# First layer of a four-layer graph network: base products kept turned for two node blocks, combined block by block

## The reference

```
weight = einsum('rb,bio->rio', w_comp, bases)      # 32 relations from 8 bases, 256 x 256 each
xw     = einsum('ni,rio->nro', h, weight)          # every node under every relation
msg    = xw[src, rel_type] * norm                  # one row of 256 per edge
out    = relu(segment_sum(msg, dst))
```

## Time and profile before

| | us |
|---|---|
| median of 3 runs | 6362.52 |
| lowest, highest | 6360.35, 6365.52 |
| span of the profiled execution | 6364.3 |

### The profile page before, as it was taken

The page is one execution under the profiler, slowest core; times in us unless marked ns, Lnnn a source line. Parts: engine busy times, 40 slices in busy tenths (PEclk is TensorE's granted clock), DMA queues, the critical chain, the costliest instruction groups (busy, mean ns, idle before and its releaser), DMA issues.

```text
span 6364.3 us, 77713 instructions
## 1 busy us (share of the span) xinstructions
PE 4985.1 (78%) x19175; PEld 3374.5 (53%) x19176; DVE 3946.2 (62%) x9442; ACT 1596.1 (25%) x3091; POOL 3597.4 (57%) x3549
## 2 busy tenths in 40 slices
PE   5999869999987777776666666279999997776766
PEld 3555547777773433333444444257787874333333
DVE  5555566666646666666666666876666665655555
ACT  3555534444440000001222222123333331000000
POOL 0000067777757777776777777223333335777776
PEclk8888889999997777777888887679999997667676
DMA  6999956666654444445777777267666774344343
GB/s 231 364 361 365 371 190 216 217 216 217 216 198 122 124 124 124 124 124 154 242 244 244 242 245 245 76 197 237 236 233 234 238 241 139 116 117 116 116 117 111
DMA packets 476381, 1279.57 MB, mean 201 GB/s; under 512 B 137938, under 2 KB 262716, under 8 KB 412533
## 3 DMA queue, kind: packets, MB, share of 16 engines
q1 hardware_dynamic: 315557, 832.27, 37.5%
q0 software_dynamic: 160464, 443.17, 24.2%
HBM read 636.68 MB, written 587.04 MB: 192 GB/s over the span
## 4 chain that ended last, share of the span: by engine, by line
PE 58%; DVE 11%; issue 10%; DMA 9%; POOL 6%; SPq 3%; ACT 1%; DVEq 1%; POOLq 0%; ACTq 0%
PE ps L1409 27%; PE ps L1584 11%; PE ps L1433 8%; PE ps L1567 5%; DMA table<-A 5%; POOL ring L630 3%; POOL A L630 2%; PE ps L1369 2%; DMA work<-place_dram 2%; DVE W L816 2%; DVE A L816 2%; PE ps L1384 1%; SPq L476 1%; SPq L355 1%; DMA A<-gat_table,ix 1%
## 5 line engine op out<-in xcount | busy, mean ns | idle before, releaser
L618 POOL DMA_INDIRECT ring<-table,idx x2490 | 2366.4, 950 | 1640.0 <-DVEq L840 774.8
L1409 PE MATMUL ps<-ring,W 128*128 128x256 f32 x3320 | 1189.5, 476 | 440.4 <-DVE W L816 278.0
L1409 PEld LDWEIGHTS ps<-ring,W 128*128 128x128 f32 x3320 | 683.3, 229 | 869.2 <-DVE W L816 399.6
L816 DVE TENSOR_SCALAR W<-iota,dloc,norm 128x128 f32<-128x128 f32 x1660 | 597.6, 361 | 766.7 <-PE ps L1409 756.8
L1409 PE MATMUL ps<-ring,A 128*128 128x256 f32 x1660 | 724.6, 543 | 271.5 <-DVE A L816 210.8
L643 POOL TENSOR_TENSOR ring<-ring,work 128x1024 f32<-128x1024 f32 x208 | 405.7, 1951 | 809.8 <-DMA ring<-rows_dram 809.8
L1584 PE MATMUL ps<-W_r,work_r 128*128 128x512 f32 x1960 | 701.1, 440 | 0.0
L834 DVE TENSOR_TENSOR X<-X,ps 128x256 f32 x1660 | 688.2, 415 | 17.2 <-PE ps L1409 15.2
L1409 PEld LDWEIGHTS ps<-ring,A 128*128 128x128 f32 x1660 | 340.2, 248 | 620.2 <-DVE A L816 367.6
L1433 PE MATMUL ps<-W_r,work_r 128*128 128x512 f32 x1568 | 560.0, 439 | 0.0
L1148 DVE TENSOR_TENSOR X<-X,ps 128x264 f32 x830 | 352.4, 425 | 329.4 <-PE ps L1567 272.8
(11 more groups left out here) (239 smaller groups left out, 7045.1 us busy)
## 6 DMA issues: line engine op xcount, KB each, us to landing
table<-A SPq DMA_DIRECT2D x294, 1024.0 KB, 6.2
ring<-rows_dram SPq DMA_DIRECT2D x208, 528.0 KB, 4.6
table<-A SPq DMA_DIRECT2D x49, 1280.0 KB, 5.4
table<-W SPq DMA_DIRECT2D x49, 1280.0 KB, 6.9
rows_dram<-ring SPq DMA_DIRECT2D x52, 1056.0 KB, 4.8
rows_dram<-A SPq DMA_DIRECT2D x52, 1056.0 KB, 4.6
ring<-table,idx POOLq DMA_INDIRECT x2490, 2.8
A<-W SPq DMA_DIRECT2D x264, 128.0 KB, 5.3
```

Of the source, the lines that this page charges most:

```text
L618: pool.indirect_dma_start(out=f_ring[:, s % NR, :], out_offset=None, in_=src, in_offset=bass.IndirectOffsetOnAxis(ap=idx[:, s:s + 1], axis ...
L816: return dve.tensor_scalar(marks_[:, k % G, :], iota[:, :], dloc[:, k:k + 1], norm[:, k:k + 1], ALU.is_equal, ALU.mult).then_inc(wk.onehot ...
L1409: pe.matmul(ps[:, s % banks, 0:D], marks_[:, s % G, :], f_ring[:, s % NR, :], start=True, stop=True).then_inc(wk.step_done, 1)
```

## The change

Two windows (called blocks) are taken together. The operands of the base product change sides: the bases are now stationary, 128 columns of them (8 bases x 2 strips of 8 output columns), and the transposed x of 256 nodes moves. The result has (strip, base, output column) along the partitions and nodes along the columns, so it is the stationary operand of the combination as it lies, and the sum over bases is along the partitions. The combination multiplies strips of 64 partitions (8 bases x 8 output columns) of one block by a 64 x 256 coefficient matrix (32 relations x 8 output columns); two strips stand beside one another. Its result has nodes along the partitions, in order. The `turns` t run over (pair of blocks, block, eighth of the output); a group of base products for the next pair follows every second turn. The split base products of nine groups are kept. There are two table tiles (A and XF); a whole one is stored in two transfers of 2 MB, with rows in node order. x comes in per pair of blocks. The seven index instructions become one.

```diff
+ OS = 8; CC = R0 * OS; OQ = D // (4 * OS); NSB = NWIN // 2; SLOTS = 9
+ l_table = [t[:, 0:R0 * D].rearrange("p (r o) -> p r o", r=R0) for t in (A, XF)]
+ L_TURNS = [(k, w, q) for k in range(NSB) for w in range(blocks_of(k)) for q in range(OQ)]
+ L_BASES = {L_AT[k, 0, 0] + (6, 8, 10, 12, 14, 16, 18, 20)[q]: (k + 1, q) for k in range(NSB - 1) for q in range(OQ)}
  # setup
- load(X[:, 0:NW1, :], x[0:NW1 * P].rearrange("(w p) c -> p w c", p=P))
-     load(comb_raw[i * BASES:(i + 1) * BASES, i // 4, i % 4 * R0:(i % 4 + 1) * R0], w_compT)
+     load(comb_row[i * OS:(i + 1) * OS, :], w_compT[i % BASES].partition_broadcast(OS))
- (six instructions on src_i, block_i, in_four, in_block)
+ ch(dve.scalar_tensor_tensor(idx[:, 0:KP], srcf[:, :], float(R0), types[:, walk0.tcol, :], ALU.mult, ALU.add))
  # SP
- sp.dma_start(l_S[k % 3][b:P:BASES, :].rearrange("i (g o) -> i g o", o=D), l_xb[:, b * D:(b + 1) * D])   # 8 per window
+ sp.dma_start(l_x[k % 2], x_rows[k]).then_inc(l_x_in[k % 2], 16)
+ def store_block(k, w):
+     t = L_AT[k, w, OQ - 1]
+     sp.wait_ge(l_act, t + 1)
+     sp.wait_ge(l_dve, t + 1)
+     for u in range(2):
+         sp.dma_start(rows[2 * k + w, u], (A, XF)[w][:, u * (R0 // 2) * D:(u + 1) * (R0 // 2) * D]).then_inc(l_t_free[w], 16)
  # VectorE (ScalarE alike: high_x, high_xb, and to_table of strip 0)
+ def low_xb(k, q):
+     m = OQ * k + q
+     dve.wait_ge(xb_high, m + 1)
+     dve.tensor_tensor(l_low[m % SLOTS], ps[:, 1 + m % 2, :]..., l_high[m % SLOTS]..., ALU.subtract).then_inc(xb_low, 1)
+ def to_table(t):
+     k, w, q = L_TURNS[t]
+     if q == 0 and k >= 1:
+         dve.wait_ge(l_t_free[w], 32 * k)
+     dve.wait_ge(l_full, 2 * t + 2)
+     dve.tensor_copy(table_place(t, 1), comb_bank(t, 1).rearrange("p (h r o) -> p h r o", h=2, o=OS)).then_inc(l_dve, 1)
+ for t, (k, w, q) in enumerate(L_TURNS):
+     to_table(t)
+     if t in L_BASES:
+         low_xb(*L_BASES[t])
+     if w == 0 and q == 4 and k + 1 < NSB:
+         low_x(k + 1)
  # PE
+ def base_products(k, q):
+     m = OQ * k + q
+     if q == 0:
+         pe.wait_ge(x_low, k + 1)
+     if m >= 2:
+         pe.wait_ge(xb_low, m - 1)
+     terms = [(b_high, l_xt_high, c) ...] + [(b_low, l_xt_high, c) ...] + [(b_high, l_xt_low, c) ...]
+     for h in range(2):
+         for n, (w, rows, c) in enumerate(terms):
+             ins = pe.matmul(ps[:, 1 + m % 2, h * 2 * P:(h + 1) * 2 * P], w[:, c, q, h, :], rows[k % 2][:, c, :], ...)
+ def combine(t):
+     k, w, q = L_TURNS[t]
+     u = (OQ * k + q) % SLOTS
+     if w == 0:
+         pe.wait_ge(xb_low, OQ * k + q + 1)
+     if t >= 2:
+         pe.wait_ge(l_act, t - 1)
+         pe.wait_ge(l_dve, t - 1)
+     terms = [(l_high, comb_high), (l_low, comb_high), (l_high, comb_low)]
+     for h in range(2):
+         for n, (rows, c) in enumerate(terms):
+             for s in range(2):
+                 part_ = slice(s * 64, (s + 1) * 64)
+                 ins = pe.matmul(comb_bank(t, s)[:, h * CC:(h + 1) * CC], rows[u][part_, h, w * P:(w + 1) * P], c[part_, :], ...)
+ for t, (k, w, q) in enumerate(L_TURNS):
+     combine(t)
+     if t in L_BASES:
+         base_products(*L_BASES[t])
+     if w == 0 and q == 3 and k + 1 < NSB:
+         turn_x(k + 1)
```

More of the change, by code:

```diff
@@ L126, in build @@
[L126 to L131, removed]
@@ L134, in build @@
+        assert 2 * CC == 512 and OQ == 8
         alpha = A[:, 0:NSC].rearrange("p (k h) -> p k h", h=HEADS)
@@ L352, in reorder_bank @@
[L352 to L369, removed]
@@ L370, in layer0_transfers, with load_x @@
-                for h in range(4):
-                    sp.wait_ge(l_t_free[h], 16 * NW1)
+                rows = table.rearrange("(w p) (t c) -> w t p c", p=P, t=2)
+                x_rows = x.rearrange("(k w p) c -> k p w c", p=P, w=2)
+                def load_x(k):
+                    if k >= 2:
+                        sp.wait_ge(l_turned, k - 1)
+                    sp.dma_start(l_x[k % 2], x_rows[k]).then_inc(l_x_in[k % 2], 16)
[5 more added lines that the diff above has]
+                        sp.dma_start(rows[2 * k + w, u], (A, XF)[w][:, u * (R0 // 2) * D:(u + 1) * (R0 // 2) * D]).then_inc(l_t_free[w], 16)
@@ L373, in head_loads @@
+                load_x(0)
+                load_x(1)
+                for k in range(NSB):
+                    if k + 2 < NSB:
+                        load_x(k + 2)
+                    for w in range(blocks_of(k)):
+                        store_block(k, w)
+                for w in range(2):
+                    sp.wait_ge(l_t_free[w], 32 * sum(blocks_of(k) > w for k in range(NSB)))
             def head_loads():
@@ L1208, in deviation @@
+                high_x(0)
+                act.wait_ge(b_split_low, 8)
+                for q in range(OQ):
+                    high_xb(0, q)
+                for t, (k, w, q) in enumerate(L_TURNS):
+                    to_table(t)
+                    if t in L_BASES:
+                        high_xb(*L_BASES[t])
+                    if w == 0 and q == 4 and k + 1 < NSB:
+                        high_x(k + 1)
             def deviation(g):
@@ new lines, in base_products @@
+                    terms = [(b_high, l_xt_high, c) for c in range(2)] + [(b_low, l_xt_high, c) for c in range(2)] + [(b_high, l_xt_low, c) for c in range(2)]
+                    for h in range(2):
+                        for n, (w, rows, c) in enumerate(terms):
+                            ins = pe.matmul(ps[:, 1 + m % 2, h * 2 * P:(h + 1) * 2 * P], w[:, c, q, h, :], rows[k % 2][:, c, :],
+                                            start=(n == 0), stop=(n == len(terms) - 1))
+                    ins.then_inc(l_xb_full, 1)
@@ new lines, in combine @@
+                def combine(t):
+                    k, w, q = L_TURNS[t]
+                    u = (OQ * k + q) % SLOTS
[5 more added lines that the diff above has]
+                    terms = [(l_high, comb_high), (l_low, comb_high), (l_high, comb_low)]
+                    for h in range(2):
+                        for n, (rows, c) in enumerate(terms):
+                            for s in range(2):
+                                part_ = slice(s * 64, (s + 1) * 64)
+                                ins = pe.matmul(comb_bank(t, s)[:, h * CC:(h + 1) * CC], rows[u][part_, h, w * P:(w + 1) * P], c[part_, :],
+                                                start=(n == 0), stop=(n == 2))
+                                if h == 1 and n == 2:
+                                    ins.then_inc(l_full, 1)
```

237 lines of the change are left out of this document (92 added, 145 removed).

## The result

| | us |
|---|---|
| changed kernel, median of 4 runs | 6325.66 (6323.48 to 6329.0) |
| kernel before, median of 4 runs beside it | 6363.64 (6360.35 to 6365.52) |
| ratio, with its 95% interval | 0.9939 (0.9927 to 0.9951) |
| span of the profiled execution after / before | 6323.4 / 6364.3 |

The change saves 38 us; the forecast was 6330. The last store of the first layer landed at 772.15 us instead of 805.1, so 33 us are made in the stage that was changed, as in the sum. The rest comes by small steps later: 37 us are saved at the end of fused and 41 at the end of the span. No stage after the first layer takes more than a few us less than before.

A forecast was written before the change was run, and what follows sets the result against it. DMA was taken to bound the kernel before (14.4 us a window), PE after (13.7 a block); 691 + 0.8 - 4 - 720.6 = -33 us gives 6330 us; likeliest 6312 to 6345, 8 in 10 within 6295 to 6410.

The forecast's parts named there:

- The pitch: PE, first-layer loop: a 256-column matmul, or pair of strips, starts every 0.118 us; bounds 0.109 and 0.125.
- Rival A: PE's pitch is the weight load's, 0.109 us: 42 us less, about 6288 us; chance 0.12.
- Rival B: The excess is per matmul, PE's pitch 0.125 us: +33 us, 6363 us, no change; chance 0.22.
- The change of mode: PE: each change between full-height and strip matmuls costs 0.095 + 0.108 = 0.203 us.
- Two turns: PE: two combining turns with their base group take 24 x 0.118 + 2 x 0.203 = 3.24 us.
- The pair of blocks: PE: sixteen turns 25.9 us, transposes of x 0.85, wait 0.6; sum 27.35 us, 13.7 per block.
- Rival C: Two strips don't run beside one another: 0.218 us per pair, +235 us, 6565; lesser form 6380 to 6410; chance 0.26 together.
- Rival D: The gain is the DMA's: 10.2 us a block would give 180 us; held forbidden by PE's count, no chance given.
- The cover: Table buffers: store 9.9 us plus about 2 to land, against 13.7; free 2 us early, gone below 370 GB/s.
- Ends and setup: First-layer stage 691 us (14.6 + 663 + 13.5) against 720.6; base split +0.8; edges earlier without x's load, -4.
- The index: Gathered row is now node x 32 + type: counted 0 for the next stage, +-3 us.
- The signs announced: Trace after: DMA share near 0.75, clock 1.0, VectorE's table wait gone, base group 1.42 us, stage's end near 772.

The follow-up runs named there:

- experiment 4: Kernel before the change with the last quarter of each window stored a second time, 1 MB more: 6489.99 us, ratio 1.0201.
- experiment 1: Changed kernel with the transposes of x for the next pair of blocks one turn earlier, right behind a base group: 6307.1 us, ratio 0.9911.
- experiment 7: Changed kernel with only 128 of 256 columns moved in every base product after the first pair of blocks: 6311.12 us, ratio 0.9905.
- experiment 6: Changed kernel with the six matmuls of strip 0 before the six of strip 1 in each combination turn: 6402.31 us, ratio 1.0049.
- experiment 8: Changed kernel with only the high x high term of each product, a third of the matmuls: 6245.55 us, ratio 0.9801.
- experiment 3: Changed kernel with a third transfer per block that stores 1 MB of the tile a second time: 6368.59 us, ratio 1.0007.
- experiment 2: Changed kernel with the old load of all of x put back into the setup, read by nothing: 6327.69 us, ratio 0.9945.

## Why the prediction was right, step by step

*What bounds.* Right on both sides. Before: DMA (experiment 4: each added byte paid in full). After: PE (experiments 1 and 7: what is taken off PE's row, 21 and 27 us, comes off the stage, 19.4 and 26.9).

*The pitch*, the number that carried the forecast: taken at 0.118, measured 0.118 for a pair of the combination and 0.120 in a base group. It came from the low-clock row, 512 columns at exactly 1.2 GHz, read as "no fixed excess", and from the remark that the load of 0.109 is barely hidden. Rival A (0.109, 6288) fell: the floor exists (0.112 in experiment 7), but 256 columns don't reach it. Rival B (0.125, 6363) fell as well; the base group, at 0.120, went 2 of 7 parts of the way to it. Neither number that the prediction took from the Trainium skill (TensorE: Matmul & The Clock Gate, sections "Back-to-back issue gap" and "Wait — 56ns, not 53.3ns?") is what the trace shows: not 0.109 for 256 columns with a load each, and not 0.124 for a pair (0.118).

*The change of mode*, 0.203: 1.63 - 12 x 0.120 = 0.19. *Two turns*, 3.24: measured 3.24. *x*: its transposes were put at 0.85 and the wait at 0.6; together 1.30 by experiment 1 against 1.45. *The pair of blocks*: 27.35, measured 27.22. Rival C fell: two strips do go side by side, and experiment 6 shows more than that. Rival D fell: PE's 13.6 a block holds the loop, and even with a third of PE's matmuls it is 12.5 (experiment 8), not 10.2. (Its price of 180 us doesn't follow from the prediction's own terms: 49 blocks at 10.2 instead of a loop of 663 make 163, and with the 33 about 196. Nothing hangs on it.)

*The cover* is the part that was argued badly, and it held by a hair. The prediction set 9.9 + 2 us for a store against 13.7 and saw 2 us free. The room is 12.8, and in the loop a half of the store lands 6.3 to 13.4 us after its issue, where alone, at the end, all of it takes 10.8: buffers are late at times, by up to 1.0 us. So the prediction's own sign of a wrong cover, first copies that wait for the store, did show, 25 times and 13 us in all, and cost PE nothing. And "the cover is gone below 370 GB/s", worked out for 4.32 MB in 11.7 us, was the wrong measure: experiment 3 moved 374 GB/s and had 130 us of waits, because 5.24 MB had to land in the same 12.8 us. The unit is the tile's cycle, not the engines' rate.

*Ends and setup.* Here two errors cancelled, and that the stage's gain came out at the predicted 33 us to the microsecond is luck.

| term | predicted | measured |
|---|---|---|
| base groups ahead of the first turn | 14.6 | 99.29 - 84.42 = 14.9 |
| turns, to the last matmul | 663 | 760.17 - 99.29 = 660.9 |
| last copies and last store | 13.5 | 772.15 - 760.17 = 12.0 |
| stage from its first base product | 691 | 687.7 |
| first base product, against 84.51 | -4 + 0.8 | -0.1 |

The loop's 2 us are 24 times the 0.13 by which the pair was shorter, 3.1, less two waits (0.49 and 0.55) for copies at its first and last turns; the tail's 1.5 are the landing. Against them stands the setup, -3.2 predicted and -0.1 measured. The edges came only 0.9 earlier (bounds of that step: 0 to 5.4), and place_dram landed 1.6 earlier; by experiment 2 the load of x alone is worth 2.2 us at the first base product, not 4. And behind the barrier the split of the bases began late: ScalarE loads its function table, 1.28 us at 76.51, ahead of the coefficients' rounding. The kernel before has the same load at 0.82 us, ahead of the wait at the barrier, where nobody waits for it; here it stands behind the wait for the coefficients. VectorE's split takes 4.91 instead of 4.63. I had counted 0.8; the stretch from the landing of place_dram to the first base product grew from 84.51 - 77.13 = 7.4 to 84.42 - 75.54 = 8.9, so 1.5, which used up the 1.6.

*The index*: 0 +-3 held. *VectorE's writes in runs of 8*: 0.69 and 0.60 us an instruction, as before (0.686, 0.596), so it was right to count nothing for them.

*The signs announced*: DMA share 0.75 at 320 GB/s (0.78 at 318), clock 1.0 (1.00), waits for the table gone (13 of 286 us left), stage's end near 772 (772.15): all seen. "A base group in 1.42" was right for twelve pitches (12 x 0.120 = 1.44); "edges landed near 34.5" was not.

What stays open: the 5 us (8 in the profiled executions) that the whole saves beyond the stage's 33. No row ties them to the change.

## What to carry to other kernels

When a change moves the bound from one engine to another, count the new bound's instructions by their pitch, and take the pitch from rows of both clock levels: here an excess that was absent at the low clock turned out not to be a fixed cost per instruction. Give each buffer its own cycle, time to fill plus time to land, and lay it beside the period of the loop, turn by turn and not on average: a tile that is handed over whole can be the bound while no engine is full. A gain promised by an earlier load needs a look at whether what comes behind it was waiting for that load at all.

## What the runs showed of the hardware

- Matmuls of two row strips run beside one another even when the program has six of one strip before six of the other: nine places 0.117 us apart for the twelve, instead of six when they alternate (experiment 6).
- With one weight load of 128 columns each, a rounded-float matmul has a pitch of 0.112 us at 128 columns (experiment 7), 0.120 at 256 and 0.232 at 512, all at the full clock; a pair of two strips, 256 columns each, has 0.118. Halving 256 columns saves 0.008 of the pitch, and 0.14 us over a group of twelve.
- ScalarE's table load (1.28 us) can fall on the critical path: it ran at 0.82 us before, ahead of the wait at the barrier and of the first real instruction (77.18), and at 76.51 after, where that instruction has a wait of its own, and behind this wait. What sets its place isn't shown. The Trainium skill (ScalarE: Activation LUTs, section "What ACT_TABLE_LOAD costs") gives 1283 ns; the trace agrees.
- One chip needed 17% more for the gathers of fused and 29% more for those of scores, and nothing more for the first layer, a stage of matmuls and large stores.
